# A two-direction Mamba layer on one core: the preparation reordered by direction, and B stored along a diagonal

## What is computed

```python
xz = x @ in_w.T
xi, z = jnp.split(xz, 2, axis=-1)
xc = silu(conv_b + sum(xp[:, k:k + L, :] * conv_w[:, k] for k in range(dc)))
dbl = xc @ xproj_w.T
dt, Bm, Cm = dbl[..., :r], dbl[..., r:r + n], dbl[..., r + n:]
delta = softplus(dt @ dt_w.T + dt_b)
dA = exp(delta[..., None] * A);  dBu = delta[..., None] * Bm[:, :, None, :] * xc[..., None]
h = dA * h + dBu;  y = einsum('bdn,bn->bd', h, C)          # five steps
out = (y + xc * D_skip) * silu(z) @ out_w.T
```

## Time and profile before

| | us |
|---|---|
| median of 3 runs (522.17 to 522.80) | 522.25 |
| the profiled execution | 521.73 |
| its span | 519.9 |
| PE busy | 466.3 |
| DVE busy | 374.2 |
| ACT busy | 233.6 |
| POOL busy | 167.3 |

### The profile page before, as it was taken

One profiled execution on the slowest core, in us unless ns is written; L12 is line 12 of the kernel. 1 busy time (PEld: TensorE's weight loads), 2 busy tenths in 40 slices (PEclk: granted clock), 3 DMA queues, 4 the chain that ended last, 5 costly groups with the idle time before them and its releaser, 6 DMA issues.

```text
span 519.9 us, 6850 instructions
## 1 busy us (share of the span) xinstructions
PE 466.3 (90%) x1798; PEld 226.2 (44%) x1798; DVE 374.2 (72%) x711; ACT 233.6 (45%) x410; POOL 167.3 (32%) x163
## 2 busy tenths in 40 slices
PE   5989999999999989899697868988889888699997
PEld 2544555555565566444454421221222222285553
DVE  0056476665665669464799897999999999678655
ACT  1112212212312221376978856888888788211100
POOL 6000100100100021402442005888989898040000
PEclk9999999999999999999869976999999999999999
DMA  9992008600000000310217563556555664510000
GB/s 266 286 281 72 1 1 261 170 1 1 0 2 0 0 1 1 95 59 0 78 39 218 149 185 98 149 161 193 168 153 151 182 190 117 158 42 12 10 10 21
DMA packets 36072, 51.75 MB, mean 100 GB/s; under 512 B 5842, under 2 KB 26606, under 8 KB 36048
## 3 DMA queue, kind: packets, MB, share of 16 engines
q1 hardware_dynamic: 34896, 50.26, 33.1%
q10 hardware_dynamic: 1152, 1.19, 0.7%
HBM read 34.59 MB, written 16.52 MB: 98 GB/s over the span
## 4 chain that ended last, share of the span: by engine, by line
PE 31%; DVE 6%; SPq 6%; ACT 5%; DMA 5%; issue 4%; ACTq 0%; DVEq 0%; POOL 0%
PE ps L1964 6%; DMA brows<-bparts 4%; PE ps L1941 4%; PE ps L948 3%; PE ps L1627 3%; PE ps L955 3%; PE ps L1578 2%; PE ps L1600 2%; PE ps L1591 2%; SPq L1448 1%; PE ps L987 1%; SPq L1517 1%; PE ps L1609 1%; PE ps L994 1%; DVE da L1803 1%
## 5 line engine op out<-in xcount | busy, mean ns | idle before, releaser
L1771 POOL TENSOR_TENSOR gb<-da,hb 128x512 f32<-128x512 f32 x62 | 77.7, 1273 | 52.9 <-ACT da L1691 46.7
L1691 ACT ACTIVATE da<-da 128x512 f32<-128x512 f32 x128 | 79.3, 631 | 23.2 <-DVE da L1803 20.9
L1803 DVE TENSOR_TENSOR da<-ps,expA 128x512 f32<-128x512 f32 x128 | 84.4, 687 | 6.2 <-PE ps L1578 5.2
L305 PE MATMUL ps<-xbuf,convw 128*128 128x384 f32 (+1 forms) x240 | 82.9, 499 | 5.3 <-DMA convw<-in_conv_wT 5.3
L359 PE MATMUL ps<-wall,peT 128*128 128x512 f32 x144 | 67.8, 593 | 0.0
L305 PEld LDWEIGHTS ps<-xbuf,convw 128*128 128x128 f32 (+1 forms) x240 | 45.8, 194 | 37.4 <-ACTq L502 3.9
L1578 PE MATMUL ps<-drows,selb 96*128 96x512 bf16 x128 | 49.2, 406 | 9.2 <-DVE da L1803 5.3
L529 ACT ACTIVATE kvs<-ps 128x512 f32<-128x512 f32 x36 | 21.5, 598 | 57.3 <-PE ps L359 57.3
L1591 PE MATMUL ps<-urows,brows 96*128 96x512 bf16 x96 | 35.8, 400 | 11.5 <-DVE gb L1810 7.8
L521 ACT ACTIVATE peT<-ps 128x384 f32<-128x384 f32 x24 | 11.8, 492 | 75.9 <-PE ps L305 75.9
L1771 POOL TENSOR_TENSOR gb<-da,gb 128x512 f32<-128x512 f32 x30 | 37.8, 1278 | 0.0
(11 more groups left out here) (233 smaller groups left out, 783.6 us busy)
## 6 DMA issues: line engine op xcount, KB each, us to landing
xbuf<-in_xT SPq DMA_DIRECT2D x11, 768.0 KB
yscr<-yst SPq DMA_DIRECT2D x28, 208.0 KB
brows<-bparts SPq DMA_DIRECT2D x16, 240.0 KB, 3.1
drows<-dparts SPq DMA_DIRECT2D x15, 192.0 KB, 2.8
dparts<-pt SPq DMA_DIRECT2D x21, 128.0 KB, 2.4
uparts<-pt SPq DMA_DIRECT2D x18, 128.0 KB, 2.4
urows<-uparts SPq DMA_DIRECT2D x16, 144.0 KB, 2.8
inw<-in_in_wT SPq DMA_DIRECT2D x2, 1024.0 KB
```

Source lines behind the costliest of these rows:

```text
L305: mm = pe.matmul(bank(T_EMB + j % 2, 0, EN), convw[0:n, k, h * P:(h + 1) * P], xbuf[0:n, q, k, c * EN:(c + 1) * EN], start=(k == 0), stop= ...
L1691: act.activation(da_at(q, j), da_at(q, j), ACT.Exp, scale=-1.0).then_inc(da_ready, 1)
L1771: pool.tensor_tensor(gb_at(q, j), da_at(q, j), state, ALU.mult).then_inc({2: m2_done, 3: m3_done, 4: m4_done}[s_], 1)
L1803: dve.tensor_tensor(da_at(q, j), bank(j % 2), expA[:, j % 2, :], ALU.mult).then_inc(e_free, 1)
```

## The change

- The items are ordered by direction: four steps of direction 0, then the rest. DVE works on items 0 and 1 before the last convolution (block 7) and on 2 and 3 behind it, starts the deltas with item 0, does `lost` and `above` of 4 and 5 between items 1 to 3, and those of 6 to 9 in one batch before item 4.
- `1 + e` of items 0 to 3 and 7 to 9 moves from ACT to DVE (`plus_one`), and so do the copies to `dbl` and `bct` of direction 0.
- xi(7) comes behind the dt products of direction 0. All ten `z` products come behind `above(6)`, all Silus of z behind the last Ln. An exp table load is put ahead of the first copy of `dtT`, another behind `high(0)`.
- PSUM banks are given out anew; `bct`'s source shares bank 7 with a dt product. The zeroing of the output banks goes.
- B: `bparts` has a pitch of 1280 + 16 in one view and 1280 in another. Its rows are zeroed whole (12 stores of 128 x 2560 bytes, which must land first), and the three parts of B are stored straight from their 16-wide form, in pieces of 32 bytes, down the diagonal; POOL's `spread` goes. `load_b` reads twelve pieces, one for each k.

The diff, cut. Of the three hand-written orders only the new side is shown (unmarked lines stay); the old orders stand in the kernel above.

```diff
-bparts = nc.dram_tensor("bparts", (NG, 12, GB, 2 * L * P), BF16, kind="Internal").ap()
+BW = 2 * L * P
+bparts = nc.dram_tensor("bparts", (12, NG, GB * (BW + NS)), BF16, kind="Internal").ap()
+brow_view = bparts[:, :, 0:GB * BW].rearrange("k g (i n) -> k g i n", n=BW)
+bdiag_view = bparts.rearrange("k g (i n) -> k (g i) n", n=BW + NS)
...
 acc = sb("acc", [P, 2, L * B], ctx=pre)
 dbl = sb("dbl", [NX, 2, L * B], ctx=pre)
...
 ITEMS = [(d, k if d == 0 else L - 1 - k) for d, k in STEPS]
 NI = len(ITEMS)
...
-XI_SLOT = [0, 1, 2, 3, 0, 1, 3, 0]
-DP_BANK = [4, 5, 6, 7, 4, 5, 4, 5, 4, 5]
-Z_BANK = [3, 6, 7, 4, 5, 6, 7, 4, 5, 4]
-XP_SLOT, BC_SLOT, CD_SLOT = [2, 0], [1, 1], [1, 3]
+XI_SLOT = [0, 1, 2, 3, 0, 1, 0, 1]
+DP_BANK = [4, 5, 6, 7, 4, 5, 6, 7, 4, 5]
+Z_BANK = [6, 7, 4, 5, 6, 7, 4, 5, 6, 7]
+XP_SLOT, CD_SLOT = [2, 2], [3, 2]
+BC_AT = [7 * 512 + 256, 7 * 512 + 256]
+BCT_AT = [2, 3]
...
     def bc(d):
-        pe.wait_ge(dbl_copied, 2 * d + 2)
         for t in range(L):
-            mm = pe.transpose(wide(BC_SLOT[d], t * NX, (t + 1) * NX), dbl[:, d, t * B:(t + 1) * B],
-                              ident[0:NX, 0:NX])
+            o = BC_AT[d] + t * NX
+            mm = pe.transpose(ps[:, o:o + NX], dbl[:, d, t * B:(t + 1) * B], ident[0:NX, 0:NX])
...
     def dt_product(n):
         d, t = ITEMS[n]
-        pe.wait_ge(dbl_copied, 2 * d + 1)
+        pe.wait_ge(dbl_copied, d + 1)
...
         xi(n)
     pe.wait_ge(xc_ready, DC)
     xp(0)
+    pe.wait_ge(acc_ready, 5)
+    xi(6)
+    pe.wait_ge(cleared, 3)
+    pe.wait_ge(bct_ready, 1)
+    dt_product(0)
+    dt_product(1)
+    bc(0)
     pe.wait_ge(acc_ready, 4)
+    dt_product(2)
+    pe.wait_ge(bct_ready, BCT_AT[0])
+    dt_product(3)
+    pe.wait_ge(acc_ready, 6)
     xi(7)
+    pe.wait_ge(diag_ready, 2)
+    pe.wait_ge(acc_ready, 7)
+    xt(0)
+    pe.wait_ge(acc_ready, 8)
+    xt(1)
+    pe.wait_ge(xc_ready, 2 * DC)
+    pe.wait_ge(rc_ready, 2)
+    xp(1)
+    pe.wait_ge(rc_ready, 4)
+    spread_c(0)
+    xt(2)
+    pe.wait_ge(dbl_copied, 3)
+    for n in (4, 5):
         dt_product(n)
     pe.wait_ge(CT_ready, 1)
     bc(1)
+    dt_product(6)
+    xt(3)
+    pe.wait_ge(bct_ready, BCT_AT[1])
+    dt_product(7)
+    pe.wait_ge(rc_ready, 5)
+    dt_product(8)
+    pe.wait_ge(rc_ready, 6)
+    dt_product(9)
+    xt(4)
+    pe.wait_ge(rc_ready, 7)
+    z(0)
+    pe.wait_ge(rc_ready, 8)
+    z(1)
+    xt(5)
+    pe.wait_ge(rc_ready, 10)
     spread_c(1)
     pe.wait_ge(CT_ready, 2)
     z(2)
     z(3)
     xt(6)
+    for n in (4, 5):
+        pe.wait_ge(z_copied, n - 3)
+        z(n)
     xt(7)
+    for n in (6, 7):
+        pe.wait_ge(z_copied, n - 3)
+        z(n)
     xt(8)
     pe.wait_ge(z_copied, 5)
     z(8)
     xt(9)
+    pe.wait_ge(z_copied, 6)
     z(9)
...
-    def copy_xp(d):
+    def copy_dt(d):
         act.wait_ge(dbl_ready, d + 1)
         act.activation(dtT[0:R, d, :], wide(XP_SLOT[d], 0, L * B, R), ACT.Copy).then_inc(dbl_copied, 1)
-        act.activation(dbl[:, d, :], wide(XP_SLOT[d], 0, L * B, NX), ACT.Copy).then_inc(dbl_copied, 1)
-
-    def copy_bc(d):
-        act.wait_ge(bc_ready, d + 1)
-        act.activation(bct[:, d, :, :].rearrange("p t n -> p (t n)"), wide(BC_SLOT[d], 0, L * NX),
+
+    def copy_second():
+        act.activation(dbl[:, 1, :], wide(XP_SLOT[1], 0, L * B, NX), ACT.Copy).then_inc(dbl_copied, 1)
+
+    def copy_bc_second():
+        act.wait_ge(bc_ready, 2)
+        act.activation(bct[:, 1, :, :].rearrange("p t n -> p (t n)"), ps[:, BC_AT[1]:BC_AT[1] + L * NX],
...
-    def softplus_terms(n):
+    def exponential_of(n):
         absolute(n)
         act.wait_ge(ab_done, n + 1)
         act.activation(ez[:, n % NZ, :], ez[:, n % NZ, :], ACT.Exp, scale=-1.0).then_inc(ez_ready, 1)
+
+    def plus_one(n):
         act.wait_ge(ez_ready, n + 1)
-        if n >= NZ:
-            act.wait_ge(delta_ready, n - NZ + 1)
         act.activation(rc[:, n % NZ, :], ez[:, n % NZ, :], ACT.Identity, bias=1.0).then_inc(one_ready, 1)
+
+    def load_exponential():
+        act.activation(warm[:, 0:1], ident[:, 0:1], ACT.Exp, scale=-1.0)
     def logarithm(n):
...
...
     conv_begin(5)
     conv_end(4)
     conv_end(5)
+    load_exponential()
     act.wait_ge(cleared, 3)
+    copy_dt(0)
     conv_begin(6)
+    for n in range(4):
+        exponential_of(n)
     conv_begin(7)
+    b_high(0)
     conv_end(6)
     conv_end(7)
+    for n in range(4):
+        logarithm(n)
+    high(0)
+    load_exponential()
+    copy_dt(1)
+    copy_second()
     copy_cd(0)
     b_middle(0)
+    exponential_of(4)
+    plus_one(4)
+    high(1)
+    exponential_of(5)
+    plus_one(5)
+    middle(0)
+    copy_bc_second()
+    b_high(1)
+    exponential_of(6)
+    plus_one(6)
+    middle(1)
+    exponential_of(7)
+    high(2)
+    exponential_of(8)
+    middle(2)
+    exponential_of(9)
+    b_middle(1)
+    logarithm(4)
+    high(3)
+    logarithm(5)
+    middle(3)
+    for n in range(6, NI):
         logarithm(n)
     copy_cd(1)
+    silu_z(0)
+    silu_z(1)
     high(4)
+    silu_z(2)
     middle(4)
+    silu_z(3)
     high(5)
+    silu_z(4)
     middle(5)
+    silu_z(5)
     high(6)
+    silu_z(6)
     middle(6)
+    silu_z(7)
     high(7)
     middle(7)
     silu_z(8)
     high(8)
     middle(8)
     high(9)
     silu_z(9)
+    load_exponential()
     middle(9)
     store(act, 9)
...
-                                  src.unsqueeze(2).to_broadcast([P, L, GB, NS]), mask4, ALU.mult)
-
     def b_rest(d):
         pool.wait_ge(bhi_ready, d + 1)
         pool.tensor_tensor(brest[:, d, :, :], bct[:, d, :, R:R + NS], bshi[:, d, :, :], ALU.subtract).then_inc(bres_ready, 1)
-        spread(bhi[:, d, :], bshi[:, d, :, :]).then_inc(bd_ready, 1)
     def b_low(d):
         pool.wait_ge(bmi_ready, d + 1)
         pool.wait_ge(bres_ready, d + 1)
         pool.tensor_tensor(bslo[:, d, :, :], brest[:, d, :, :], bsmi[:, d, :, :], ALU.subtract).then_inc(bslo_ready, 1)
-        spread(bmi[:, d, :], bsmi[:, d, :, :]).then_inc(bd_ready, 1)
-        pool.wait_ge(bslo_ready, d + 1)
-        spread(blo[:, d, :], bslo[:, d, :, :]).then_inc(bd_ready, 1)
     def c_spread(d):
...
...
                       ALU.mult, ALU.add).then_inc(xnT_copied, 1)
...
+    def copy_first():
+        dve.wait_ge(dbl_copied, 1)
+        dve.tensor_copy(dbl[:, 0, :], wide(XP_SLOT[0], 0, L * B, NX)).then_inc(bct_ready, 1)
+
+    def copy_bc_first():
+        dve.wait_ge(bc_ready, 1)
+        dve.tensor_copy(bct[:, 0, :, :].rearrange("p t n -> p (t n)"),
+                        ps[:, BC_AT[0]:BC_AT[0] + L * NX]).then_inc(bct_ready, 1)
+
     def c_dot_b(d):
-        dve.wait_ge(bct_ready, d + 1)
+        dve.wait_ge(bct_ready, BCT_AT[d])
         ch.link(dve.tensor_tensor(cbp[:, d, :, :], bct[:, d, :, R:R + NS], bct[:, d, :, R + NS:NX], ALU.mult))
         return ch.mark(dve.tensor_reduce(cb[:, d, :], cbp[:, d, :, :], AX.X, ALU.add))
+
+    def plus_one(n):
+        dve.wait_ge(ez_ready, n + 1)
+        dve.tensor_scalar(rc[:, n % NZ, :], ez[:, n % NZ, :], 1.0, None, ALU.add).then_inc(one_ready, 1)
     def lost(n):
...
...
+    for n in range(6):
+        conv_middle(n)
+    copy_first()
+    conv_middle(6)
+    copy_bc_first()
+    for n in range(2):
+        plus_one(n)
+    for n in range(2):
+        lost(n)
+    for n in range(2):
+        above(n)
+    plus_one(2)
+    conv_middle(7)
+    plus_one(3)
+    for n in (2, 3):
+        lost(n)
+    for n in (2, 3):
+        above(n)
+    ch.upto(c_dot_b(0))
     delta_(0)
     u_(0)
     for n in range(NI):
+        if n not in (3, NI - 1):
             delta_(n + 1)
         rest(n)
+        if n not in (3, NI - 1):
             u_(n + 1)
+        if n == 2:
+            lost(5)
         skip_(n)
+        if n == 2:
+            above(5)
         low(n)
+        if n == 1:
+            lost(4)
+            above(4)
+        if n == 3:
+            cb_done = c_dot_b(1)
+            lost(6)
+            plus_one(7)
+            above(6)
+            plus_one(8)
+            lost(7)
+            lost(8)
+            above(7)
+            plus_one(9)
+            above(8)
+            lost(9)
+            above(9)
+            ch.upto(cb_done)
+            delta_(4)
+            u_(4)
...
 def load_b(sp, g, q):
-    sp.dma_start(brows[:, q], bparts[bass.ds(g, 1)].rearrange("g k i n -> (g k i) n")).then_inc(u_landed[q], 16)
+    sp.dma_start(brows[:, q], brow_view[:, bass.ds(g, 1)].rearrange("k g i n -> (k g) i n")).then_inc(u_landed[q], 16)
...
     def store_b(d):
-        sp.wait_ge(bd_ready, 3 * (d + 1))
-        for k, src in enumerate([bhi, bhi, bhi, bmi, bmi, blo]):
-            sp.dma_start(bparts[:, 2 * k + d, :, d * L * P:(d + 1) * L * P], src[:, d, :]).then_inc(b_stored, 16)
+        sp.wait_ge(bslo_ready, d + 1)
+        for k, src in enumerate([bshi, bshi, bshi, bsmi, bsmi, bslo]):
+            own = bdiag_view[2 * k + d, :, d * L * P:(d + 1) * L * P]
+            sp.dma_start(own.rearrange("b (t p) -> b t p", p=P)[:, :, 0:NS],
```

(100 more changed lines are left out.)

52 lines of the change are left out of this document (3 added, 49 removed).

## The result

| | before | after |
|---|---|---|
| median of 20 runs each, us | 521.91 | 525.76 |
| ratio, 95% interval | | 1.0051 [1.0026, 1.0076] |
| the profiled execution, us | 521.73 | 528.18 |
| its span, us | 519.9 | 526.4 |

The change made the kernel slower by 0.5%. The forecast was 518.7 us, 0.7% faster; the chance given to slower was 0.20. The ratio leaves out runs that lie more than 1.5% above the fastest of their kernel, which are five of the 20 after, the profiled one among them; the median of the other 15 is 524.56 us. The profiled execution of after lies 2.4 us above the median of all its runs, so its 6.5 us of span are more than what the change costs as a rule.

A forecast was written before the change was run, and what follows sets the result against it. The preparation was bound by the time item 9 is stored, after which the DVE-paced scan follows. Terms -7.1 + 1.6 + 0.8 + 1.2 = -3.5 us, from the median 522.25, gave 518.7 us; range 515.0 to 524.5.

The forecast's parts named there:

- Term 1: Preparation, new engine order: item 9's stores land at 301.7 against 308.82, so -7.1 us.
- seven plus_one at 0.6 = 4.2 us: DVE in the preparation: added `plus_one` work of 4.2 us, four of the seven lying in earlier idle time.
- Off the path: POOL's six removed products of 1.4 us and more in the preparation: their removal was credited with no gain.
- the timetable: Walk of the engines' new orders through the preparation: `delta_(0)` at 247.6, z(9) ending 294.6, last `skip_` 296.2.
- the wait of low(3): DVE's low(3) waits for item 0's stores, landing at 265.9 behind B's packets; otherwise it would start at 265.1.
- Term 2: PE's clock halves after idling from 264.9 to 268.0, slowing two z products: +1.6 us (0 to +4).
- Term 3: B's 32-byte store packets, 35 ns each, delay item 0's landing and low(3): +0.8 us (0 to +7.0).
- lower bound of 18 ns: Cheapest price of a 32-byte store packet of B, taken from small reads; it would make the delay 0.
- The slower rival: Slow packets: B's small stores delay item 0's landing and low(3), giving 525 to 527 us; chance 0.2.
- Term 4: Loads of B in the scan, as twelve pieces: 0.2 us in six pairs of groups, +1.2 us (0 to 3).
- two more of 2 x 60 ns: Load of `brows`: rows come eight to an engine instead of six, 0.24 us longer, double beside other loads.
- The 1 us that the prediction took for measurable: Whole kernel: about 1 us, 0.2%, is what a measurement can tell from no change.

The follow-up runs named there:

- experiment 4: The changed kernel with B's rows issued first of a group's five loads instead of last, early zeroing of `drows` kept: 524.48 us, ratio 1.0065 to the kernel before.
- experiment 7: The changed kernel with B stored and loaded the old way and POOL's memset of `drows` after the last `above`: 520.16 us, ratio 0.9981 to the kernel before.
- experiment 10: The changed kernel with each of the two early memsets of `drows` issued as eight of 256 columns: 525.32 us, ratio 1.0107 to the kernel before.
- Experiment 1: The changed kernel with POOL zeroing the unused rows of `drows` only after the last `above` (the late memset): 520.07 us, ratio 0.9972 to the kernel before.
- Experiment 5: The kernel before with a 128-byte gap between the twelve parts of a group of B, so twelve pieces per load: 524.89 us, ratio 1.0064.
- experiment 2: The changed kernel with B stored and loaded the old way, POOL's products back, memset still early: 519.76 us, ratio 0.9973 to the kernel before.
- experiments 5 and 6: The kernel before with gaps in B's store: between its twelve parts, 524.89 us; 16 bytes behind each of 96 rows (ninety-six pieces), 521.94 us, ratio 1.0009.
- experiment 8: The changed kernel with old storage of B, late memset, and xi(7) moved ahead of the dt products: 521.55 us, ratio 0.9996 to the kernel before.

## Why the prediction was wrong

**Term 1, the new order (-7.1 us): right sign, wrong on what it left out.** In experiment 4, with the early memset, item 9 lands 76.2 us after the first copy of `dtT`, against 76.6 before: 0.4 us are won where terms 1 to 3 said 4.7. With the memset out of the way the last `above` ends 1.4 us later than forecast (274.4 against 273.0), and item 9 lands at 302.31 + 2.44 = 304.75, 4.1 us earlier than before. But some 2 of the 4.1 come from POOL's missing products, which no term held. The order with the late memset and the old storage of B (experiment 7) lands at 303.73 + 2.74 = 306.47, 2.4 us earlier, where terms 1 and 2 said 5.5. The first step that failed is "seven plus_one at 0.6 = 4.2 us". They take 4.2 us with the memset late, but 7.3 beside it. That the 4.2 agrees is luck: five of the seven take 0.42 each, and the first two 2.09 together, since the first stands beside a product of POOL. The prediction looked at POOL's wait ahead of `drows` only for whether POOL comes late, not for what POOL's work does to DVE while it runs. The new order put DVE's most urgent batch, on which all ten z wait, beside it.

**"Off the path" for POOL's six products: wrong.** Their going is worth 1.9 us in the old order (70.9 to 69.0) and 1.9 in the new (67.5 to 65.6). It was a gain that the prediction did not count, and it hides part of the loss.

**Missed in term 1: item 6's landing.** high(9) waits for it, at 303.86 after 1.32 us of idle time; the timetable held only the wait of low(3). The Silu of z(9), whose product had ended at 303.4, starts at 304.40 for it, so 1.0 us of it reaches the end:

```profile
303.86 0.63 ACT L1145 ACTIVATE pt<-du 128x512 bf16<-128x512 bf16 x1 [1.32 <-DMA uparts<-pt]
```

The late memset keeps a wait of 1.05 us there. It is the wait that a faster preparation meets next.

**Term 2, the clock (+1.6): mis-sized.** The forecast fall came from 264 to 271 in experiment 4, as the prediction has it, but from 259 to 272 in the execution profiled after. The one from 238 was not foreseen at all, in a stretch where PE shows no gap. A third, behind the stall, is in the traces of after and of experiment 10 and not in experiment 4. (The term's own sum, two times 1.31 less 0.9, is 1.7 and not 1.6, and the timetable's z(9) adds up to 294.3, not 294.6.) That xi(7) took 4.63 us, and not the 2.2 of the timetable, is 2.4 us by itself, about the 2.0 us by which `delta_(0)` is later than forecast. Experiment 1 keeps two falls (0.57 from 238 to 242, 0.53 from 262 to 270) and loses the third.

**Term 3, small packets (+0.8; 0 to 7): nothing.** The stretch 254 to 264 of the kernel after (packets, MB, share of 16 engines; then KB and us to landing):

```profile
q1 hardware_dynamic: 4221, 0.39, 28.7%
...
bparts<-bshi SPq DMA_DIRECT2D x3, 20.0 KB, 2.0
```

0.287 x 10 us x 16 / 4221 is 11 ns of one engine a packet, the larger packets of the stretch included. That is below the lower bound of 18 ns, and low(3) waited for nothing. The slower rival had the right sign by the wrong mechanism. The rule of the Trainium skill, "DMA: Bandwidth & Descriptors", Specifications, that below 512 B the engine does a read-modify-write, does not show as a price in these numbers.

**Term 4, the load of B (+1.2; 0 to 3): the mechanism stood there, the price was too low.** By the row price the load was to be 0.2 us longer; it is 0.4 to 0.9 longer (3.93 to 4.23 us against 3.11 to 3.69 in the chains) and its issue 0.54. PE's waits grow by 2.9 us in five pairs, and 0.9 us more stands at group 1: 3.8 us, above the upper end of the bracket. Experiment 5 gives it alone as 0.64% of 521.2 us, 3.3 us. The failed step is "two more of 2 x 60 ns": it took packets from the rows of another transfer, where the engines in use were the quantity, and left SP's issue out.

The range (515.0 to 524.5) ends 1.3 us below the median of all runs. Its upper part was made of slow packets alone; a second way to lose was not in it. The 1 us that the prediction took for measurable was too little as well: the intervals here reach 1.3 to 2.4 us to each side.

## What to carry to other kernels

Before an operation is moved, list what POOL does in its new place: a DVE operation can take 1.8 us for 0.7 beside a product, or 3.5 for 0.4 beside a memset, and if a batch that feeds PE is hit, the clock can come on top. Large POOL memsets belong where DVE's work is not urgent, and splitting them does not help. When a layout is chosen for a cheap store, look at the outer size of each load it leaves: 96 rows at one pitch, gaps or not, cost nothing; 12 parts cost 10 to 28% more time to landing and half a microsecond more to issue, sixteen times. No version here beats the kernel before by more than the measurement is uncertain: the late memset (0.9972) and the old storage in the new order (0.9973) come nearest. A layout with B on the diagonal and 96 rows at one pitch was not tried.

## What had not been expected of the hardware

- A DVE TENSOR_SCALAR of 128x512 f32 takes 0.41 us, less than the 0.68 of the two-input operations, but it takes 3.55 beside POOL's two memsets of 3.54 together, and 4.10 beside sixteen pieces of 0.30. Beside a product of POOL it takes 1.67 (experiment 2, at 239.33). The two-input operations beside the same memset keep their 0.68, but stretch beside POOL's products. In the kernel before both stand next to each other, and POOL's product is stretched as well, 2.39 us where the others take 1.40:

```profile
271.05 1.89 DVE L1317 TENSOR_TENSOR du<-rc,ez 128x512 f32<-128x512 f32 x1
272.87 1.21 DVE L1336 TENSOR_TENSOR res<-du 128x1024 f32<-128x1024 f32 x1
274.00 0.68 DVE L1327 TENSOR_TENSOR du<-du,ps 128x512 f32<-128x512 f32 x1
...
270.01 2.39 POOL L1235 TENSOR_TENSOR blo<-bslo,maskb 128x640 bf16<-128x640 bf16 x1
272.34 3.54 POOL L1753 MEMSET drows<- 48x2048 bf16 x2
```

- Stores in 32-byte pieces to HBM: 11 ns of one engine a packet, averaged over all packets of that stretch, and 2.0 us to landing for 20 KB.
- A load of 96 rows in twelve parts sends four small packets fewer than the same rows at one pitch (5778 against 5842 under 512 B in 16 loads), lands after 3.83 us against 2.90 (experiments 5 and 6) and costs SP 864 ns an issue against 317.
- The granted clock fell to 0.50 at 238 with PE shown busy throughout the 10 us before (9.88 of 10.00), among fp32 products of 33 rows, and in experiment 8 it fell from 241 with PE busy up to 243.
